# A fused attention and MLP kernel: Wo and half of W1 are split in earlier groups, kept in memory and fetched back; the last results are finished tile by tile

## What is computed

```python
q = (seq2 + b_self) @ Wq + bq
k = concat([x + b_prev, seq2 + b_self]) @ Wk + bk
v = concat([x, seq2]) @ Wv + bv
score_prev = where(mask, q @ k[:l1].T * SCALE, -inf)
score_self = (q * k[l1:]).sum(-1) * SCALE
w = softmax(concat([score_prev, score_self], -1))
y = x + (w[..., :-1] @ v[:l1] + w[..., -1:] * v[l1:]) @ Wo + bo      # 512 x 512
h = gelu(y @ W1 + b1)                                                # 512 -> 2048
out = y + concat([h @ W2 + b2, h @ We[idx] + be[idx]], -1)           # 384 + 128 columns
```

## Time and profile before

| what | us |
|---|---|
| three runs | 1793.42, 1796.44, 1796.46 (median 1796.44) |
| the profiled execution | 1807.21 |
| its span, first to last instruction | 1805.1 |
| TensorE busy in the span | 1719.9 |
| VectorE, ScalarE, GpSimd busy | 942.4, 709.5, 663.4 |

### The profile page before, as it was taken

How to read it: one execution, slowest core, us unless ns; L and a number is a source line. 1 busy time by engine, 2 the same in 40 slices (tenths; PEclk the granted TensorE clock), 3 DMA queues, 4 the chain that set the end, 5 groups by cost and what they waited for, 6 DMA issues and landing times.

```text
span 1805.1 us, 27962 instructions
## 1 busy us (share of the span) xinstructions
PE 1719.9 (95%) x8256; PEld 1262.1 (70%) x8256; DVE 942.4 (52%) x1430; ACT 709.5 (39%) x1259; POOL 663.4 (37%) x521
## 2 busy tenths in 40 slices
PE   6998999999999999999987899999999999999996
PEld 5765656666666666666652688888888888888885
DVE  4577576775866768757587643232232323232321
ACT  3253454444544445445344443323232323233222
POOL 3165577584874847748564301000010101010101
PEclk8999999999999999999996999999999999999998
DMA  6452444443534435244344342223131413232212
GB/s 143 76 114 51 91 103 107 86 97 73 120 90 91 96 85 119 69 103 87 80 110 121 109 122 50 68 48 86 46 87 41 87 52 75 61 66 72 47 30 53
DMA packets 370269, 149.45 MB, mean 83 GB/s; under 512 B 289226, under 2 KB 329162, under 8 KB 370194
## 3 DMA queue, kind: packets, MB, share of 16 engines
q1 hardware_dynamic: 364966, 146.28, 35.7%
q10 hardware_dynamic: 5228, 2.35, 0.5%
HBM read 70.41 MB, written 27.28 MB: 54 GB/s over the span
## 4 chain that ended last, share of the span: by engine, by line
PE 78%; issue 6%; DVE 5%; DMA 4%; SPq 3%; POOL 2%; ACT 1%; ACTq 0%; DVEq 0%; POOLq 0%
PE ps_proj L1258 14%; PE ps_max L1289 6%; PE ps_av L1210 6%; PE ps_av L1212 6%; PE ps_av L1211 6%; PE ps_av L1329 6%; PE ps_score L1316 5%; PE ps_proj L1210 3%; PE ps_proj L1211 3%; PE ps_proj L1212 3%; DMA stacks<-parts 3%; PE ps_score L1210 3%; PE ps_max L1212 3%; PE ps_score L1212 3%; PE ps_max L1210 3%
## 5 line engine op out<-in xcount | busy, mean ns | idle before, releaser
L729 ACT ACTIVATE p_f<-ps_score 128x512 f32<-128x512 f32 x512 | 303.8, 599 | 459.2 <-PE ps_score L1316 414.8
L941 DVE TENSOR_REDUCE m_col<-ps_max 128x1 f32<-128x512 f32 x512 | 328.7, 683 | 201.2 <-PE ps_max L1289 199.9
L604 POOL TENSOR_TENSOR p_sum<-p_sum,p_f 128x512 f32<-128x512 f32 x256 | 335.4, 1342 | 3.3 <-ACT p_f L729 3.3
L644 POOL TENSOR_TENSOR z_f<-z_f,a_raw 128x512 f32<-128x512 f32 x32 | 40.8, 1287 | 750.5 <-ACT z_f L842 730.0
L1135 DVE TENSOR_TENSOR h_lo<-h_f,h_hi 128x512 fp32r<-128x512 f32 x128 | 88.0, 687 | 412.2 <-ACT h_hi L833 412.1
L601 POOL TENSOR_TENSOR p_sum<-p_f 128x512 f32<-128x512 f32 x128 | 161.6, 1293 | 210.7 <-PE ps_av L1338 205.4
L1289 PE MATMUL ps_max<-stacks 97*128 97x512 f32 x512 | 189.3, 437 | 38.1 <-DVE m_col L941 19.4
L1258 PE MATMUL ps_proj<-in_hi,w_hi 128*128 128x512 f32 x512 | 207.8, 406 | 11.2 <-POOL in_lo L609 7.9
L1316 PE MATMUL ps_score<-stacks 99*128 99x512 f32 x512 | 209.0, 419 | 5.6 <-ACT p_f L729 5.4
L1210 PE MATMUL ps_av<-y_hi,w_hi 128*128 128x512 f32 x512 | 199.9, 390 | 6.6 <-ACT h_hi L833 3.8
L1258 PE MATMUL ps_proj<-in_lo,w_hi 128*128 128x512 f32 x512 | 205.6, 402 | 0.0
(11 more groups left out here) (122 smaller groups left out, 2729.1 us busy)
## 6 DMA issues: line engine op xcount, KB each, us to landing
stacks<-parts SPq DMA_DIRECT2D x384, 128.0 KB
raw<-in_x_dram SPq DMA_DIRECT2D x128, 64.0 KB, 2.3
raw<-in_fside_BxSxS_dram SPq DMA_DIRECT2D x128, 64.0 KB, 2.2
den<-own_scratch SPq DMA_DIRECT2D x128, 64.0 KB, 2.8
attn_scratch<-num SPq DMA_DIRECT2D x32, 256.0 KB, 3.0
x_raw<-in_x_dram SPq DMA_DIRECT2D x128, 64.0 KB, 2.2
we_raw<-in_L_cond_We_dram SPq DMA_DIRECT2D x32, 256.0 KB, 2.8
resid_scratch<-a_raw SPq DMA_DIRECT2D x32, 256.0 KB, 2.0
```

What stands on the lines that cost most here:

```text
L604: pool.tensor_tensor(p_sum[:, j], p_sum[:, j], now, ALU.add).then_inc(sum_made, 1)
L729: act.activation(p_f[:, i % FLIGHT], ps_score[i % 2][:, :], ACT.Exp, scale=SCALE).then_inc(p_made, 1)
L941: dve.tensor_reduce(m_col[:, n % C, n // C:n // C + 1], ps_max[n % 2][:, :], AX.X, ALU.max).then_inc(max_made, 1)
```

## The change

Tiles 0 to 7 are now split in groups (0,2) and (0,3), tiles 8 to 11 in (7,0), in slots 10 to 13: ScalarE casts into `turned`, VectorE subtracts in place in `raw`, SP stores both parts in `wide_scratch` and fetches them into place later: Wo at the start of (7,2), tiles 4 to 7 at its end, 8 to 11 between the loads of x in (7,3). Normalizing group (7,2) moves out of (7,3), behind the first `y_low`s. The third quarter of the first We is split at row 3 in place of row 1. In the last b the residual stays in SBUF; TensorE finishes the four accumulators one after the other, and VectorE adds bias and residual in one instruction, transposes, and SP and ScalarE's queue store two quarters of each tile each.

```diff
+        first_split_at = {(2 + n // C, 10 + n % C): n for n in range(2 * C)}
+        last_split_at = {(0, 10 + n): 2 * C + n for n in range(C)}
+            def split_load(n):
                 sp.dma_start(raw[:, n % 4], wide_source(n)).then_inc(wide_landed[n % 4], DMA)
+            def split_keep(n):
+                sp.wait_ge(split_lo_made, n + 1)
+                sp.dma_start(wide_dram[n, 0], turned[:, n % 4]).then_inc(split_kept, DMA)
+                sp.dma_start(wide_dram[n, 1], raw[:, n % 4]).then_inc(split_kept, DMA)
+            def wide_fetch(n):
+                hi, lo = wide_parts(n)
+                sp.dma_start(f(hi), wide_dram[n, 0]).then_inc(wide_fetched[n // C], DMA)
+                sp.dma_start(f(lo), wide_dram[n, 1]).then_inc(wide_fetched[n // C], DMA)
...
+                    if first and g == 2:
+                        sp.wait_ge(turn_made, 2 * C * 2)
+                        for n in range(C):
+                            split_load(n)
...
+                    if last and g == 2:
+                        sp.wait_ge(v2_mm, C * B)
+                        for n in range(C):
+                            wide_fetch(n)
...
+                        attended(0, 3)
+                        residual(0, 1)
+                        for n in (8, 9):
+                            wide_fetch(n)
+                        residual(0, 2)
+                        for n in (10, 11):
+                            wide_fetch(n)
+                        residual(0, 3)
                         wide_late(EARLY)
...
+                    if first and g >= 2:
+                        for n in range(C * (g - 2), C * (g - 1)):
+                            split_keep(n)
...
+                    if last and g == 2:
+                        for n in range(C, 2 * C):
+                            wide_fetch(n)
...
+            def split_high(n):
+                act.wait_ge(wide_landed[n % 4], DMA * (n // 4 + 1))
...
+                act.copy(turned[:, n % 4].bitcast(F32R), raw[:, n % 4]).then_inc(split_hi_made, 1)
...
+            def split_low(n):
+                dve.wait_ge(split_hi_made, n + 1)
+                dve.tensor_tensor(raw[:, n % 4].bitcast(F32R), raw[:, n % 4], turned[:, n % 4],
+                                  ALU.subtract).then_inc(split_lo_made, 1)
...
-                    if first and m < 2:
-                        expert_high(b, m + 1, True)
+                    if first and m in (0, 3):
+                        expert_high(b, 1 if m == 0 else 2, True)
...
+            def end_sum(c):
+                dve.wait_ge(end_mm, c + 1)
+                dve.wait_ge(whole_made, C * B)
...
+                dve.scalar_tensor_tensor(out=end_z[:, c], in0=ps_out[c][:, :], scalar=bias_2[:, c:c + 1],
+                                         in1=end_whole[c], op0=ALU.add, op1=ALU.add).then_inc(end_made, 1)
+                dve.wait_ge(end_made, c + 1)
+                dve.transpose(end_z_t[:, c], end_z[:, c]).then_inc(z_t_made, 1)
...
+            for n in range(4):
+                one_over_den(B - 1, C - 2, n)
+            normalize(B - 1, C - 2)
             hidden_low(0, 0)
...
+            def end_outputs():
+                for m, c in ((KH - 2, 0), (KH - 2, 1), (KH - 1, 0), (KH - 1, 1),
+                             (KH - 2, 2), (KH - 1, 2), (KH - 2, 3), (KH - 1, 3)):
+                    if c == 0:
+                        pe.wait_ge(h_lo_made, KH * (B - 1) + m + 1)
```

More of the change, by code:

```diff
@@ L467, in batch @@
                         wide_late(EARLY + 2)
-                        attended(0, 3)
-                        residual(0, 1)
-                        residual(0, 2)
-                        residual(0, 3)
-                    if not (first and g == 0):
-                        store(*after(b, g, -1))
+                    if not (first and g == 0) and not (last and g == C - 1):
+                        store(*after(b, g, -1))
+                    if first and g >= 2:
+                        for n in range(C * (g - 2), C * (g - 1)):
+                            split_keep(n)
+                    if last and g == 0:
+                        for n in range(2 * C, EARLY):
+                            split_keep(n)
+                    if last and g == 2:
+                        for n in range(C, 2 * C):
+                            wide_fetch(n)
+                if first:
+                    sp.wait_ge(split_kept, 2 * 2 * C * DMA)
             batches(sp, batch)
@@ L512, in result, with end_result @@
                                  ).then_inc(stored[c % 2], DMA)
+            def end_result(c, quads):
+                sp.wait_ge(z_t_made, C * (B - 1) + c + 1)
+                for q in quads:
+                    sp.dma_start(blocks(out, B - 1, c, q),
+                                 end_z_t[QUAD * q:QUAD * (q + 1), c].rearrange("p (tb f) -> p tb f", f=QUAD)
+                                 ).then_inc(stored[c % 2], DMA)
             sp.wait_ge(ids_landed, DMA)
@@ L523, in _ @@
             w2_piece(3)
+            store(B - 1, C - 2)
             store(B - 1, C - 1)
@@ L539, in rows @@
                     expert_weights(b, 3)
+                if last:
+                    for c in range(C):
+                        end_result(c, (0, 1))
+                    return
                 if not last:
@@ L646, in rows @@
             def rows(b, first, last):
-                for c in range(C):
+                for c in range(C if not last else 0):
                     add_residual(b, c)
@@ L793, in batch @@
                             q_out(*nxt2)
+                        if first and (g, i) in first_split_at:
+                            split_high(first_split_at[g, i])
+                        if last and (g, i) in last_split_at:
+                            split_high(last_split_at[g, i])
                         if last:
-                            for n in wide_at.get((g, i), ()):
-                                wide_high(n)
                             for c in attended_at.get((g, i), ()):
@@ L878, in rows @@
                         y_high(b + 1, c)
-                for c in range(C if last else 2):
-                    result(b, c)
+                    for c in range(2):
+                        result(b, c)
+                else:
+                    for c in range(C):
+                        end_result(c, (2, 3))
             batches(act, rows)
@@ L1077, in batch @@
                             own_less_max(*nxt)
-                        if i in (13, 14) and started:
+                        if i in (13, 14) and started and not (last and g == C - 1):
                             for n in range(2) if i == 13 else range(2, 4):
@@ L1082, in batch @@
                             qk(*nxt2)
-                        if i == 15 and started:
+                        if i == 15 and started and not (last and g == C - 1):
                             normalize(*after(b, g, -1))
+                        if first and (g, i) in first_split_at:
+                            split_low(first_split_at[g, i])
+                        if last and (g, i) in last_split_at:
+                            split_low(last_split_at[g, i])
                         if last:
-                            for n in wide_at.get((g, i), ()):
-                                wide_low(n)
                             for c in attended_at.get((g, i), ()):
@@ L1200, in rows @@
                         y_low(b + 1, c)
-                for c in range(C if last else 2):
-                    turn_result(b, c)
+                for c in range(C):
+                    if last:
+                        end_sum(c)
+                    elif c < 2:
+                        turn_result(b, c)
             batches(dve, rows)
@@ L1463, in rows @@
                         hidden(b, m + 2, range(C), first)
+                    if last and m == KH - 2:
+                        end_outputs()
+                        break
                     outputs(b, m, first)
```

82 lines of the change are left out of this document (52 added, 30 removed).

## The result

The changed kernel takes **1800.22 us** (median of 13 runs, 1798.07 to 1802.12), the kernel before 1795.43 on the same chips (13 runs, 1789.31 to 1801.08). The ratio is 1.0026 with a 95% interval of 1.0018 to 1.0035: slower by 0.26%, 4.8 us by the medians, a little over what such a measurement can tell from no change. The forecast was 1797.0 with a range of 1784 to 1809.

What follows compares the result with a forecast made beforehand. TensorE was taken as the bound, busy 1719.9 of 1805.1 us, the rest mainly waits and slow clock. The terms 21 - 4.5 + 0 - 3 - 5 - 8 = +0.5 on the median 1796.4 gave 1797 us, range 1784 to 1809.

Steps and rivals of the forecast that it cites:

- The splits: Groups (0,2), (0,3), (7,0): splits make VectorE 6 us late, TensorE waits; 7 us each with slow clock, +21.
- The lower bound: Splits' groups: if GpSimd never held a split, casts alone put VectorE 4 us back; 9 us in all.
- The upper bound of 36: Splits' groups: one split held until GpSimd's row of sums ends adds 7 us; 36 in all.
- The credit for `normalize`: Group (0,2): the splits remove the held `normalize`, 8.9 us in the profile, credited at half: -4.5 (0 to -8.9).
- (7,1), 0: `normalize` in (7,1) keeps its place and neighbours: 0 (down to -7).
- The passage: (7,2), (7,3) to MLP start: splits gone save 3, fetches eat 2, numerator wait falls 2: -3 (-6 to +4).
- rival 3: Passage: fetches delay the attention and x tiles, first output projection starts 5 us later: 1802 us; chance 0.10.
- We: Start of the MLP: TensorE's 3.75 us gap for a gelu goes, with its slow clock: -5 (-3 to -5.5).
- The end: After the last matmul: finishing tiles in turn shortens the tail, DMAs setting the finish: -8 (-6.5 to -9).
- Rival 1: Splits' groups: VectorE has room, 3 us a group; held waits also in ordinary runs: 1780.5 or 1785 us; chance 0.28.
- Rival 2: Slots 10 to 13, splits' groups: a split held until GpSimd's row ends: 1810 or 1806 us; chance 0.25.
- Rival 4: The end: TensorE's last tiles in another order could wait 0.3 us for `h_lo`; inside the range, no chance given.

Runs made afterwards that it cites:

- `base_again`: The kernel before, unchanged, run again for a second profile: 1796.68 us, ratio 0.9999 to the kernel before.
- `low_out`: The changed kernel without the twelve split subtractions on VectorE and its wait for their casts: 1783.07 us, ratio 0.9933 to the kernel before.
- `casts_early`: The changed kernel with ScalarE's twelve casts up to four slots earlier, subtractions where they are: 1798.83 us, ratio 1.0016 to the kernel before.
- `end_only`: The kernel before with the new end and nothing else: 1789.66 us, ratio 0.9968.
- `fetch_late`: The changed kernel with the eight fetches of W1's first half behind the last attention tile and x tiles: 1793.01 us, ratio 0.9989 to the kernel before.
- `spread`: The changed kernel with splits in other slots of (0,2), (7,0), (7,2), W1's fetches behind the last attention tile: 1777.77 us, ratio 0.9898 to the kernel before.
- `we_only`: The kernel before with We's third quarter split at row 3 and nothing else: 1791.88 us, ratio 0.9983.

## Why the forecast was right, and where it was not

The time was in the range and on the right side of the middle, and most of the mechanism was as described. But it was near partly by luck, through errors that cancel. Term by term, against a kernel before without held multiplications (`base_again`):

- **The splits, +21 forecast, +18.0 measured** (4.64 + 6.45 + 4.94 + 1.96), 16.3 and 17.1 by the medians of two kernels. Against `low_out`, which has no fall of the clock in (1,0), the slow clock at its start adds 1.6, which makes 19.4. The step by step working was right: VectorE late by 5.5 us in place of 6, subtractions of 0.75 to 1.7 us beside GpSimd, TensorE waiting for the maxima and then at the slow clock. (The 923.3 of the working takes the fourth split at its least, 0.6; it took 0.75.) What was sized a little high is the wait: 3.7 to 4.7 us for each group, not 5. The lower bound, that the casts alone would still put VectorE 4 us back, wasn't tested: `casts_early` takes the casts away and leaves GpSimd. The estimate given there, 4.4 us from the denominator's end (914.9) to that of a third subtraction that nothing holds, speaks for it. The upper bound of 36 doesn't follow from its text: 7 us more for one split make 28, for one in each group 42. None was held that long.
- **The credit for `normalize`, -4.5 forecast, 0 measured.** This is the step that failed. I had the 10.8 us between the profile and the median, priced the two held multiplications at 16, concluded that the usual run "doesn't hold all of both", and credited half of the one in (0,2). That took the rest of the profiled execution to be like the median. It wasn't: by the table the two cost 14.2 us (nearly 16, as priced, since `base_again` has a fall of the clock in (0,2) and that execution has none), and everything else in it was 3.8 us shorter than in `base_again`, so that the 10.8 left nothing for the usual run. None of the eight places in the four profiles was held.
- **(7,1), 0**: right, its `normalize` took 1.63 us; the +1.96 in that group is the slow clock behind the gap ahead of it.
- **The passage, -3 forecast, -1.4 measured** (a step that `end_only`, with no change there, shows too: -1.25). The net is near and both of its parts were far too small. Freed of the splits and with the attention tile first, the passage gains 7.6 us; the eight fetches ahead of that tile take 6.2 of them back, 3.32 as TensorE's wait and the rest with the slow clock behind it. I had 5 (3 and the 2 of the numerator) and 2. The reason against rival 3, "SyncE reaches them earlier than before", was true and not enough. The length of the transfer was right: from the issue of the first fetch (981.96) to the use of the tile (992.51) are 10.5 us, where I had 10. What was wrong is that it would eat only 2. Counted from the first maximum for (7,3), the tile is issued after 39.5 us in the kernel before (first profile), 33.3 in the changed one and 32.7 in `fetch_late`, and ScalarE starts on it after 42.3, 39.9 and 35.7: with 2 MB under way ahead of it, it gives back 4.2 of the 6.6 us.
- **We, -5 forecast, -3.5 to -4.6 measured**: the gap went, as said, and what was late next cost 0.2 to 0.5 us.
- **The end, -8 forecast, -7.35 measured** (-7.79 and the 0.44 of the later last matmul); by the runs of `end_only` 5.7, between 3 and 8.4. The DMAs did not set it as I said: the sixteen stores were issued from 1787.2 on, each queue took 0.75 us for one of its eight (5.95 and 6.05 us), and the DMA engines were 0.84 busy at 115 GB/s, not 0.91 at 167. The end comes 3.5 us after the last of them is issued; the forecast's "1 to 1.5 us to complete" is a term that no run shows by itself. So here the issuing of two queues and the engines are near each other, and that two queues "don't help" was not shown.

The sum: 18.0 + 0 - 1.4 - 4.6 - 7.35 = +4.6, and the medians say +4.8. That they agree so closely is luck: the profile of the changed kernel is only 1.9 us longer than `base_again`, and the other 2.8 us stand in the rows up to (0,2), (1,0) and the loop, where the falls of the clock differ. Had the first term been kept and the credit left out, the forecast would have been 1801.4.

**The rivals.** Rival 1 (VectorE has room) fell by the gaps of 3.7 to 4.7 us, as its sign said. Rival 2 (a split held until GpSimd's row ends) didn't come: none of the twelve took over 1.7 us, though in `spread` one took 2.58 in slot 7 of (0,2). Rival 3 (the fetches starve the passage) came: its sign was a wait of over 3 us for `a_lo`, and that was 3.32. I had it as a case beside the forecast, with 0.10 and 5 us on top; it was the forecast's own -3 that hid it, because it cut the gain, not the time. Rival 4 was real with its 0.3 us (0.44).

The Trainium skill ("SBUF — State Buffer", section "Who interferes with whom") says that whoever issues first has the shared ports for the whole instruction. By that rule VectorE would wait for the one GpSimd instruction in progress. All subtractions of the changed kernel agree with it, 0.75 to 1.7 us beside sums of 1.3 to 1.75. The 8.98 and 8.95 us of the first profile don't, and they are not alone: a `normalize` of 2.64 us in the same profile (at 1006.18), of 2.38 in `base_again`, of 2.70 in `we_only`, and the subtraction of 2.58 in `spread` each waited over the end of one GpSimd instruction and the whole of the next. All six ended 0.54 to 0.56 us after GpSimd's row of instructions had ended, and not at a boundary inside it. Why these and not the many others that began beside such a row stays open. What appeared at these two places in one execution of several was taken for a property of the place.

## What to carry to other kernels

Before an edit is credited with a stall that it removes, see whether the stall is in the ordinary run: one profile that stands 10.8 us above the median holds things that the median doesn't, and a second profile settles it. For work that is to be hidden, the share of an engine that is idle says little; list the slots and read in each how long it is idle *before* the next thing that another engine waits for: twelve splits cost 16 to 19 us between the denominator and the next maxima, and eight of them about 1.5 us some slots ahead. And when a transfer is put ahead of one that a critical instruction needs, in the same queue, it must be counted against that instruction with its whole length, even if the net looks like a gain: here the order of the DMAs alone was worth 7 us.

## What the runs showed of the hardware that was not expected

**Luck with the clock.** In every profile TensorE's clock falls to the 1.2 GHz level, mostly for 3.4 us, three to six times in the six batches of the loop, nearly always at the same place of the batch. The waits just ahead of it are short, 0.46 and 0.30 us in the case shown, and `low_out` has the same two (0.46 and 0.28) and no fall. One such place in `base_again`, and about the same place in `low_out`:

```profile
486.00:491.00 5.00, 4.82 (x14) 3.81 (x15) 2.48 (x4) 0.60 (x1) 5.00 (x5) 0.66 0.00 0
```

```profile
482.00:487.00 5.00, 4.52 (x17) 2.95 (x17) 4.33 (x8) 1.46 (x3) 5.00 (x5) 1.00 0.00 0
```

A fall costs 1.5 to 1.6 us, and it is there in one execution and not in another: the steps of the loop in the table (-1.89, +2.61) are one or two of these more or fewer. It is likely most of why runs of one kernel differ by 5 us: in the twelve runs of `end_only`, those with a mean granted clock of 0.982 have a span of 1785.4 to 1786.1, those with 0.977 or 0.978 one of 1790.0 to 1796.8. A difference of 1.4 us, as that of the earlier casts, is found in a profile's steps and not in twelve runs.

**A DMA behind a backlog.** A tile of 256 KB took 3 us from issue to use in `fetch_late`, with no other 256 KB transfer issued in the 3.8 us ahead of it, and 6.6 behind eight of them, while the engines ran at 1.02 busy and 275 GB/s. That is more than the 203 GB/s that the forecast had taken as the rate of a busy stretch.
